# Cross-attention with FP4 feed-forward on one core: from scores that are transposed after the exponential to two passes of scores, with a transposed bias seeded in PSUM

## What is computed

```python
q = (layernorm(x) @ w_q.T + b_q).reshape(B, T, H, D)      # B=8, T=S=512, H=D=16
k = (ctx @ w_k.T + b_k).reshape(B, S, H, D)
v = (ctx @ w_v.T + b_v).reshape(B, S, H, D)
scores = einsum('bthd,bshd->bhts', q * D**-0.5, k) + attn_bias
scores = where(key_padding_mask, NEG_INF, scores)
x = x + (einsum('bhts,bshd->bthd', softmax(scores), v)) @ out_proj_w.T + out_proj_b
h = silu(fp4_linear(layernorm(x), w_gate)) * fp4_linear(layernorm(x), w_up)
x = x + fp4_linear(h, w_down)
```

## Time and profile before

| | us |
|---|---|
| median of 3 runs | 1030.16 (1028.19 to 1031.83) |
| the profiled execution | 1029.46 |
| its span, first to last instruction | 1027.5 |

### The profile page before, as it was taken

The page is one execution under the profiler, slowest core; times in us unless marked ns, Lnnn a source line. Parts: engine busy times, 40 slices in busy tenths (PEclk is TensorE's granted clock), DMA queues, the critical chain, the costliest instruction groups (busy, mean ns, idle before and its releaser), DMA issues.

```text
span 1027.5 us, 23032 instructions
## 1 busy us (share of the span) xinstructions
PE 952.6 (93%) x6612; PEld 667.7 (65%) x6612; DVE 857.5 (83%) x2125; ACT 722.0 (70%) x1685; POOL 198.6 (19%) x156
## 2 busy tenths in 40 slices
PE   5299999999999999999999999978778999999997
PEld 3176666666657666665765766645456878878885
DVE  3287988888888888888888878899757999999996
ACT  2298988877888888888788888856634555555542
POOL 3222232140240213114024121245400000000000
PEclk9699999999999999999999999999979999999999
DMA  9553451451533335055153433611000000000000
GB/s 290 134 124 76 113 124 27 121 138 28 120 101 90 84 103 123 15 129 132 36 115 93 103 75 89 145 35 31 2 0 6 17 16 15 21 16 15 20 16 26
DMA packets 47339, 76.14 MB, mean 74 GB/s; under 512 B 10016, under 2 KB 26784, under 8 KB 47264
## 3 DMA queue, kind: packets, MB, share of 16 engines
q1 hardware_dynamic: 47264, 75.34, 29.3%
HBM read 20.78 MB, written 4.19 MB: 24 GB/s over the span
## 4 chain that ended last, share of the span: by engine, by line
PE 82%; DVE 8%; issue 5%; SPq 2%; ACT 2%; DMA 1%; DVEq 1%; POOL 0%; ACTq 0%; POOLq 0%
PE psum L967 24%; PE psum L1099 14%; PE psum L1056 12%; PE psum L1235 9%; PE psum L1217 4%; PE psum L1219 4%; PE psum L1218 4%; PE psum L988 3%; PE psum L995 3%; PE psum L1013 2%; PE psum L982 2%; DVE att L845 2%; DVE att L764 2%; SPq L367 1%; SPq L378 1%
## 5 line engine op out<-in xcount | busy, mean ns | idle before, releaser
L569 ACT ACTIVATE att<-att,neg_max 128x512 f32<-128x512 f32 x512 | 367.3, 719 | 119.1 <-DVE neg_max L845 111.9
L845 DVE CUSTOM_DVE_ANT_0 att<-psum,att 128x512 f32<-128x512 f32 x512 | 346.7, 686 | 106.2 <-PE psum L1099 94.2
L967 PE MATMUL psum<-ident,att 128*128 128x128 f32 x2448 | 364.7, 275 | 19.9 <-DVE att L764 7.4
L967 PEld LDWEIGHTS psum<-ident,att 128*128 128x128 f32 x2448 | 298.0, 141 | 94.6 <-issue 45.6
L1099 PE MATMUL psum<-stack 128*128 128x512 f32 x512 | 273.1, 535 | 26.4 <-DMA stack<-kl 17.3
L1099 PEld LDWEIGHTS psum<-stack 128*128 128x128 f32 x512 | 96.7, 189 | 141.4 <-DVE neg_max L845 81.3
L764 DVE COPY att<-psum 128x512 f32<-128x512 f32 x256 | 175.6, 686 | 3.7 <-PE psum L967 3.7
L1056 PE MATMUL psum<-att 128*32 128x256 f32 x2048 | 164.0, 393 | 2.0 <-issue 2.0
L608 ACT ACTIVATE att<-psum 128x512 f32<-128x512 f32 x256 | 150.5, 588 | 18.1 <-PE psum L967 13.1
L1235 PE MATMUL psum<-att 128*128 128x256 f32 (+1 forms) x384 | 98.0, 388 | 2.8 <-ACT att L649 2.8
L569 ACT ACTIVATION_READ_ACCUMULATOR att<-att,neg_max 128x1 f32 x512 | 96.9, 189 | 0.0
(11 more groups left out here) (96 smaller groups left out, 1043.7 us busy)
## 6 DMA issues: line engine op xcount, KB each, us to landing
stack<-qh SPq DMA_DIRECT2D x128, 128.0 KB, 2.4
stack<-ql SPq DMA_DIRECT2D x128, 128.0 KB, 2.3
att<-in_fside_1xSxS_dram SPq DMA_DIRECT2D x16, 512.0 KB, 3.7
stack<-kh SPq DMA_DIRECT2D x128, 64.0 KB, 2.0
stack<-kl SPq DMA_DIRECT2D x128, 64.0 KB, 2.0
att<-in_ctx_dram SPq DMA_DIRECT2D x8, 512.0 KB, 4.8
out_dram<-att SPq DMA_DIRECT2D x32, 128.0 KB, 1.7
x<-in_x_dram SPq DMA_DIRECT2D x1, 3584.0 KB, 20.4
```

Source lines behind the costliest of these rows:

```text
L569: act.activation(prob[:, slot, :], prob[:, slot, :], ACT.Exp, bias=neg_max[:, slot:slot + 1], scale=-1.0, accum_out=row_sum[:, o, tt * 8 + ...
L845: dve.tensor_tensor_reduce(out=prob[:, slot, :], in0=ps_score[:, bank_of(j)[0], :], in1=bias_m[:, tt, :], scale=-1.0, scalar=BIG, op0=ALU. ...
L967: return pe.transpose(out_, in_, ident[:, :])
```

## The change

The attention is written anew; the feed-forward layer's steps stay.

- **Pass A.** A period has 16 *steps*: 2 heads (r = 0, 1) and 128 query rows. TensorE makes the two score tiles [t, s] with 48 contraction rows each, one from partition 0, one from partition 64. VectorE adds bias and takes the maximum as before, and throws the sum away (`waste`). This pass only yields the maximum. The stack has 3 blocks of 16 rows per head.
- **The maximum.** For each half period (a *quad*, 4 heads, 8 steps; 32 quads) VectorE splits the maxima into high and low (`split_m`), TensorE transposes them (`make_mT`), VectorE takes them to `m_row` (`take_mT`, at step 1 and step 9), and SyncE copies them into two further rows of the q stack, 2 partitions x 128 numbers at a time (`stack_m`, 16 transfers). The k stack has ones there.
- **Pass B**, `LAG = 12` steps later. The scores are made again, transposed, [s, t], from 50 rows: with the rows of the maximum they come out reduced by it. The PSUM banks have been filled with the transposed, masked bias before, and the matmul adds to it (`start=False`). ScalarE fills 6 of 8 units (`seed_unit`, an ACT copy of 128 x 1024), TensorE 2 of 8 (two identity products with `bias_high` and `bias_low` for each bank, four matmuls a unit). ScalarE takes the exponential of 128 x 1024 straight out of PSUM, with no bias and no row sum. So the probabilities need no transpose: `transpose_prob` and both `take_prob` are gone.
- **Values**: 4 column strips with 512 moving columns, one round of four for two steps. The row sums come out of a column of ones in `vpad`. Output is taken to SBUF (`take_O`), transposed (`make_ot`), multiplied by the reciprocal (`normalise`) and transposed back (`make_oT`). `expand_inverse` and `make_r` are gone.
- **SyncE**: `stack_q` and `stack_k` issue 12 transfers of 16 partitions each, four times in a period in all, `stack_m` 16 transfers twice in a period.
- The transposed bias is made once (16 transposes at the start); POOL adds the mask to it for each batch and splits half of it. POOL also applies the layernorm. The last weight pieces are prepared after the attention's last step.

The core of the diff, `-` before, `+` after:

```diff
@@ SyncE
-            def stack_q(n_oct, o, n_tiles_free):
-                for j in (0, 2, 1, 3):
...
-                    for k in range(4):
-                        sp.dma_start(q_stack[o][rows, k, :, :].bitcast(F32), (qh, ql, qh, ql)[j][src, :, :].bitcast(F32)).then_inc(stacked[o], 16)
+            def stack_q(m, slot, h):
+                for part in range(2):
+                    wait(sp, (q_high, q_low)[part], m + 1)
+                    plain(sp)
+                    for kk in range(2):
+                        for r in range(2):
+                            head = slice(64 * h + 32 * kk + 16 * r, 64 * h + 32 * kk + 16 * r + 16)
+                            for i in ((0, 1), (2,))[part]:
+                                rows = slice(64 * r + 16 * i, 64 * r + 16 * i + 16)
+                                sp.dma_start(q_stack[rows, slot, kk, :].bitcast(F32), (qh, ql)[part][head, :].bitcast(F32)).then_inc(stacked[slot], 16)
+            def stack_m(quad, slot):
+                sp.wait_ge(mT_taken, quad + 1)
+                plain(sp)
+                for r in range(2):
+                    for kk in range(2):
+                        for tt in range(NT):
+                            row = 16 * r + 8 * kk + 2 * tt
+                            sp.dma_start(q_stack[64 * r + 48:64 * r + 50, slot, kk, tt * P:(tt + 1) * P].bitcast(F32),
+                                         m_row[row:row + 2, :].bitcast(F32)).then_inc(m_stacked, 16)
...
+                if not (first and o == 0):
+                    stack_m(2 * n - 1, 2 * (1 - o) + 1)
...
+                    stack_q(n + 1, 2 * (1 - o), 0)
+                if o == 0:
+                    stack_k(n + 1, 2 * (1 - o), 0)
+                stack_m(2 * n, 2 * o)
+                if o == 1 and not last:
+                    stack_k(n + 1, 2 * (1 - o), 0)
...
+                    stack_q(n + 1, 2 * (1 - o) + 1, 1)
+                    stack_k(n + 1, 2 * (1 - o) + 1, 1)
@@ TensorE
+            def scores(n, o, s, r):
+                wait(pe, biased, t - 1)
+                rows = slice(64 * r, 64 * r + 48)
+                pe.matmul(ps_A[:, r, :], q_stack[rows, 2 * o + h, kk, tt * P:(tt + 1) * P], k_stack[rows, 2 * o + h, kk, :],
+                          start=True, stop=True).then_inc(score_ready, 1)
+            def unit(n, o, s, r):
+                if r == 1:
+                    if bu == 0:
+                        pe.wait_ge(m_stacked, 256 * (2 * m + h + 1))
...
+                rows = slice(64 * r, 64 * r + 50)
+                last = pe.matmul(ps_B[:, 2 * (s % 2) + r, :], k_stack[rows, slot, kk, c * P:(c + 1) * P], q_stack[rows, slot, kk, :],
+                                 start=False, stop=True, skip_group_check=True)
...
+                    scores(n, o, s, 0)
+                    if has_b:
+                        unit(n, o, s, 1)
+                        unit(n, o, s, 0)
+                    scores(n, o, s, 1)
+                    if has_b:
+                        rounds(n, o, s)
...
+                        if s == 4:
+                            pe.wait_ge(q_taken, n + 2)
+                            make_k(1, 0, ps_misc)
@@ VectorE, in a step
+                    for r in range(2):
+                        dve.tensor_tensor_reduce(out=waste[:, r, :], in0=ps_A[:, r, :], in1=bias_m[:, tt, :], scale=-1.0,
+                                                 scalar=BIG, op0=ALU.add, op1=ALU.min,
+                                                 accum_out=nm[:, h, col:col + 1]).then_inc(biased, 1)
+                            if s == 1 and not (first and o == 0):
+                                take_mT(2 * n - 1)
+                            if s == 9:
+                                take_mT(2 * n)
+                            if o == 0 and s == 5:
+                                high_q(n + 1, 1, 384 * (b + 1))
@@ ScalarE
+                act.activation(probT[:, c % 2, 2 * kk:2 * kk + 2, :], pair_of(s), ACT.Exp).then_inc(exp_ready, 1)
...
+                act.activation(pair_of(s), bias_mT[:, c, :].unsqueeze(1).to_broadcast([P, 2, S]), ACT.Copy).then_inc(seeded_act, 1)
```

More of the change, by code:

```diff
@@ L388, in body, with period @@
+            sp.wait_ge(ones_ready, 1)
+            for h in range(2):
+                stack_q(0, h, h)
+                stack_k(0, h, h)
+            def period(b, o):
+                first, last = is_first(b), is_last(b)
+                n = 2 * b + o
+                if o == 0 and not last:
+                    wait(sp, tc_ready, 2 * b + 2)
                     plain(sp)
-                    sp.dma_start(ctx_n[:, :, :], ctx_v[:, one(nb)].rearrange("p o t e -> p (o t) e")).then_inc(ctx_in, 16)
+                    sp.dma_start(ctx_n[:, :, :], ctx_v[:, one(b + 1)].rearrange("p o t e -> p (o t) e")).then_inc(ctx_in, 16)
@@ new lines, in period @@
+                stack_m(2 * n, 2 * o)
+                if o == 1 and not last:
+                    stack_k(n + 1, 2 * (1 - o), 0)
+                if o == 0 or not last:
+                    wait(sp, st_ready, 16 * n)
+                    plain(sp)
+                    stack_q(n + 1, 2 * (1 - o) + 1, 1)
+                    stack_k(n + 1, 2 * (1 - o) + 1, 1)
+                if o == 1 and not last:
+                    for tt in range(NT):
+                        sp.wait_ge(biased, n * TILES + 2 * (QSTEPS + 2 * tt + 2))
@@ L516, in _ @@
+            def body(b):
+                period(b, 0)
+                period(b, 1)
             batches(pool, body)
-            expand_inverse(2 * B - 1)
+            for q in range(3, PIECES):
+                weights_piece(q)
             rstd2_of(B - 1)
@@ L1047, in _, with weights_free @@
-            place = {}
-            def values(o, u, c, units):
-                half, r = u // 2, u % 2
-                if c == 0:
-                    pe.wait_ge(T_even, 4 * (units + 1))
-                    pe.wait_ge(T_odd, 4 * (units + 1))
-                for k in range(4):
-                    last = pe.matmul(ps_O[32 * k:32 * k + 32, half * 2 * P:(half + 1) * 2 * P], vpad[:, o, c, 2 * k + r, :],
-                                     probT[:, u % 2, k, c, :], start=(r == 0 and c == 0), stop=(r == 1 and c == SC - 1))
-                if c == SC - 1:
-                    last.then_inc(pv_ready, 1)
+            def weights_free(q):
+                pe.wait_ge(gwT_taken, q + 1)
+                pe.wait_ge(gw_low, min(q + 1, IC))
@@ new lines, in seed_unit @@
+            def seed_unit(n, s, batch):
+                m, h, bu = unit_of(n, s)
+                if SEED_BY[bu] != "T" or not live_unit(m):
+                    return
+                c = bu // 2
+                pe.wait_ge(blow_ready, 2 * batch + c // 2 + 1)
+                wait(pe, exp_ready, STEPS * n + s - LAG - 1)
+                for r in range(2):
+                    bank = ps_B[:, 2 * (s % 2) + r, :]
+                    pe.matmul(bank, ident_r[:, :], bias_high[:, c // 2, :], start=True, stop=False, skip_group_check=True)
+                    pe.matmul(bank, ident_r[:, :], bias_low[:, c // 2, :], start=False, stop=False, skip_group_check=True)
@@ new lines, in values @@
+            def values(m, o, h, c):
+                quad = 2 * m + h
+                pe.wait_ge(exp_ready, 8 * quad + 2 * c + 2)
+                if c == 0:
+                    wait(pe, O_taken, quad)
+                    if h == 0:
+                        pe.wait_ge(v_taken, 2 * m + 2)
+                for j in range(4):
+                    last = pe.matmul(ps_O[32 * j:32 * j + 32, :], vpad[:, o, c, 4 * h + j, :], probT[:, c % 2, j, :],
+                                     start=c == 0, stop=c == SC - 1)
+                last.then_inc(round_done, 1)
```

1068 lines of the change are left out of this document (616 added, 452 removed).

## The result

| | before | after |
|---|---|---|
| median of 4 runs, us | 1029.18 (1027.60 to 1031.83) | 1415.77 (1413.43 to 1421.11) |
| ratio, 95% interval | | 1.376 (1.371 to 1.381) |
| span of the profiled execution, us | 1027.5 | 1412.7 |
| mean granted TensorE clock | 0.983 | 0.808 |

The change makes the kernel 386 us slower. 1415.77 us lies over the forecast of 1215 and over the upper end of its range, 1300.

The account below looks back on a forecast made before the run. SP's queue, with 80 transfers a period, and TensorE's waits for landed maxima were to bound the changed kernel: start 77.4, seven batches 758, last quads 67, then 36 and 274 make 1213, with 2.0 more 1215 us; range 1095 to 1300.

Parts of the forecast that it names:

- q and k at 0.635: SP's queue: each 16-partition transfer of the q and k stacks holds it for 0.635 us, as SBUF to SBUF bursts did.
- Two-row transfers at 0.50: SP's queue: each 2-partition transfer of the maxima holds it for 0.50 us, the middle of 0.37 and 0.635.
- the formula: Attention batch: 84 q or k transfer prices plus 64 maxima transfer prices plus 23 us, 108.3 us in sum.
- Halves of the array run side by side: TensorE: score and unit matmuls in different row halves overlap, 2 x 0.32 us a step instead of 4 x 0.32.
- A step of 2.2 us: Attention: the engines would allow 2.2 us a step, 35 us a period, from TensorE's sum of 35.5 us.
- Bias, ctx and mask at 2.6 us: SP's queue, a batch's fourth quad: six loads at 0.4 us and their waits take 2.6 us.
- two-row transfers nearly free: Rival, SP's queue: maxima transfers cost 0.2 us each, a batch 89.5 us, in all 1065 us; chance 0.13.
- transfers cheap, engines bound, faster: Rival, SP's queue: all transfers cost 0.37 us, a batch 83 us, in all 1009 us; chance 0.15.
- The rival in which TensorE alone bounds (1085): Attention: row halves don't overlap and SP keeps up, 45.8 us a period, in all 1085 us; chance 0.07.
- The ends: Outside the seven batches: start 77.4 us, last three quads 67, then 36 to the first gate product, 274 to the end.
- The signs that I had set: Profile after: SP without gaps over most of a batch, TensorE idle before units in 31 or 32 pieces of 4 us and more.
- Its cheap case (0.56 and 0.37): Lower bound of the same mechanism on SP's queue: q and k transfers at 0.56 us, maxima's at 0.37, giving 1102 us.

Follow-up runs that it names:

- floor: Kernel after with takes_first and bias_early, and the cut transfers of light (output not the reference's): 1081.94 us.
- takes_first: Kernel after, whole computation, with ScalarE's take copies of each step put ahead of the step's exponential: 1362.8 us.
- light: Kernel after without 15 of 16 transfers of each quad's maxima and 10 of 12 of each q and k stack (output not the reference's): 1215.13 us.
- m_one: Kernel after without 15 of the 16 transfers of each quad's maxima, q and k transfers kept (output not the reference's): 1324.31 us.
- qk_few: Kernel after without 10 of the 12 transfers of each stack of q and of k, maxima's transfers kept (output not the reference's): 1292.67 us.
- bias_early: Kernel after, whole computation, with the next batch's four bias loads put ahead of the last 12 k transfers on SP's queue: 1390.13 us.
- both: Kernel after, whole computation, with bias_early and takes_first together: 1335.64 us.
- no_a_takes: Kernel after without pass A, the maximum, its transfers and the bias reloads, copies put ahead of the exponential: 963.23 us, ratio 0.934 to the kernel before.

## Why the prediction was right in sign and wrong in size

By its own steps:

1. *Direction and first cause: right.* The change is slower, and SP's 80 transfers a period on one queue served in order are the largest part of it (-201 us when they are taken away).
2. *q and k at 0.635: right.* 0.63 in the batch above, and the queue shows it at the start as well (12 from 19.52 to 27.20).
3. *Two-row transfers at 0.50: too low, 0.61.* Taking the middle between two far rows was the error; the rows of the same kind, SBUF to SBUF, were the right ones. With 0.61 the formula gives 84 x 0.635 + 64 x 0.61 + 23 = 115.4 us a batch, 7 us more. That is 49 us in the seven batches and some 7 us in the other quads.
4. *Halves of the array run side by side: right.* Score and unit start within 0.01 us of each other (438.50 and 438.51), and the next pair 0.35 us on at full clock (442.77 to 443.12). The rival in which they don't is refuted.
5. *A step of 2.2 us: wrong, and the costliest step.* It was the sum of the busiest engine's work, and so took it that the engines never wait for each other. The sum itself was near: 71 us a batch for TensorE, 77.1 busy in `floor` at a clock of 0.94. The step was not: 3.7 us in the median here, 2.6 even in `floor`. The quads that the forecast gave 23.2 and 22.0 us last 32.0 and 31.2, since SP stands there until enough steps have made the maxima. What the step holds beyond the sum: a chain of unit, exponential, copy, product, with 1.7 us of TensorE's idle time in it (-53 us when cut, and more of it with a light queue), and a lower clock. Values of 512 columns, put at 0.9 us, take 1.07 at full clock and 1.93 at half. How much of the excess each has isn't settled: no run here holds the clock up while the order stays. A hint is that the same 4489 matmuls are busy for 1029.0 us in the kernel after, 992.3 in `takes_first` and 920.0 in `floor`, though ends of matmuls are modelled.
6. *Bias, ctx and mask at 2.6 us: wrong by kind.* I priced their issue on SP. What counts is what waits behind their landing: POOL's additions, then VectorE's first maximum and `normalise`, then TensorE's `make_mT`, 15.3 us idle in the batch shown. The quad lasts 40.8 us, not 33.5. Moving the loads gave 26 us; `floor` still waits 60.9 us at `make_mT`, half of it (30) between batches.
7. *The rival "two-row transfers nearly free": refuted* by 0.61. That case leant on a row of another kind. The page "DMA: Bandwidth & Descriptors" of the Trainium skill, section on why a DMA increments its semaphore by 16, gives such a transfer, by its rule, 2 engines. No run shows on how many it ran; its issue, 0.61 us against 0.63, is hardly cheaper.
8. *The rival "transfers cheap, engines bound, faster" (0.15): refuted twice.* The price isn't cheap, and with nearly no transfers the kernel has 1215 us, not 1009. That the light run gives the forecast's number is chance. The rival in which TensorE alone bounds (1085) falls with point 4.
9. *The ends.* First maxima landed by 68.24 + 9.79 + 2 = 80.0 (forecast 77.4); the last three quads 1085.02 - 1002.04 = 83.0 (67); from the last landing to the first gate product 1136.13 - 1096.7 = 39.4 (36); from there on 276.6 (274). The sum of the misses is 2.6 + 176 (seven batches) + 16 + 3.4 + 2.6 = 200 us: nine tenths of it are in the batches. Point 3 is 56 of the 200; the rest of the batches is points 5 and 6.

The signs that I had set came out mixed. SP was to show no gaps over most of a batch: it has 33 of 137.5 us, short of the third that was to mean wrong. TensorE's gaps ahead of the unit matmuls came in 19 pieces and 61.1 us, 3.2 us each, not in 31 of 4 us and more. Both said that SP wasn't alone. The upper end of the range, 1300, took the prices of transfers at their dearest and the engines at their quickest; the two are independent, and the range should have had the step's price in it too. Its cheap case (0.56 and 0.37) comes to 1098 us by the forecast's own formula, not to 1102, which changes nothing.

That the parts are in a row and not in parallel is borne out by the sums, of one execution each: m_one and qk_few add up to `light`, bias_early and takes_first to `both`, each of them shortens the kernel, and the two edits of order turn some of what they save into the wait for landed maxima. They aren't independent, though: the two edits of order give 133 us with the light queue and 80 with the full one. What isn't settled: how the step's excess splits between clock and waits, and what the 200 us would be if the transfers of `stack_m` were issued from another queue, which wasn't tried.

## What to carry to other kernels

Count the transfers that a change issues on a queue and multiply by the issue price of the same kind of transfer in the trace, whatever their size. Don't take a step's time from the busiest engine's sum where engines hand tiles to each other in fixed orders: follow one chain of hand-overs around, and put short copies that another engine waits for ahead of long operations that wait themselves. A pass of its own for the maximum should be priced by itself first: here it turned 0.93 of the old time into 1.30 (`no_a_takes` against `both`, each with the copies moved; 1.33 in `takes_first`).

## What the runs showed of the hardware

The page's line for the two-row transfers (issue min/median/max ns, first and last start):

```profile
L403 SPq DMA_DIRECT2D q_stack<-m_row x512: 562/563/672, 68.2 to 1094.1; - x171
```

- A transfer of 2 partitions and 1.0 KB holds SP's queue for 0.563 us in the median, and one of 16 partitions and 32 KB for 0.589 (L381). 32 times the bytes add 0.03 us. What comes from HBM holds it for less: 0.40 us for ctx, 0.34 for the mask (563.52 and 564.16 in the kernel after).
- Matmuls in the two halves of the array's rows start within 0.01 us of each other; a pair of them follows the last after 0.35 us at full clock (442.77 to 443.12) and 0.59 at half (447.19 to 447.78).
- Values in four column strips take 1.07 us for 512 columns in eight records at full clock, 1.93 at half.
- The granted clock falls from 1.00 to 0.50 within 3 us behind many of TensorE's stops of 1.6 to 1.8 us (445.27 in the kernel after, 719.60 in `light`), but not behind all: behind those that end at 582.38 and 589.57 in the kernel after, of 1.77 and 1.75 us, it stays at 1.00. It is 0.81 over the kernel after, 0.87 in `light`, 0.92 in `floor`, 0.98 before.
